# Adding up a body's weighed rows on TensorE, one body later

## The reference

```
comp  = h[src] + rel_emb[rel_id]              # one row of 128 per edge, 474 kinds of relation
score = sum(comp * h[dst], axis=-1)
ex    = exp(score - segment_max(score, dst)[dst])
norm  = ex / segment_sum(ex, dst)[dst]
neigh = segment_sum(comp * norm[:, None], dst)
x     = x + tanh(neigh @ neigh_w)
```

## Time and profile before

| | us |
|---|---|
| median of 3 runs | 10201.28 (10199.97 to 10209.77) |
| the profiled execution | 10194.69 |
| its span, first to last instruction | 10192.9 |
| the last layer's loop, 116 bodies | 8763 to 10131 |

### The profile page before, as it was taken

The page is one execution under the profiler, slowest core; times in us unless marked ns, Lnnn a source line. Parts: engine busy times, 40 slices in busy tenths (PEclk is TensorE's granted clock), DMA queues, the critical chain, the costliest instruction groups (busy, mean ns, idle before and its releaser), DMA issues. The chain is left out here.

```text
span 10192.9 us, 223970 instructions
## 1 busy us (share of the span) xinstructions
PE 6724.1 (66%) x64938; PEld 5458.5 (54%) x64939; DVE 7705.4 (76%) x22255; ACT 5834.0 (57%) x12496; POOL 6563.4 (64%) x5757
## 2 busy tenths in 40 slices
PE   3893986366665666656666478778878876466665
PEld 2882985254554554545555355555555533466664
DVE  9779776477776777767777699989989931677776
ACT  4224226366665666646666389979979920355543
POOL 0777750277776777767777568768858811666665
PEclk8555556578877788877888799999999988777777
DMA  0110115432222322223222212112112264222222
GB/s 23 55 45 15 60 41 197 145 52 53 53 53 44 52 53 53 52 45 52 53 53 53 49 47 59 52 47 59 52 46 59 59 209 162 47 46 46 46 46 44
DMA packets 422026, 630.49 MB, mean 62 GB/s; under 512 B 275527, under 2 KB 332321, under 8 KB 398217
## 3 DMA queue, kind: packets, MB, share of 16 engines
q0 software_dynamic: 192432, 385.10, 18.1%
q1 hardware_dynamic: 162096, 158.87, 5.0%
q10 hardware_dynamic: 67401, 85.32, 2.4%
HBM read 527.43 MB, written 103.02 MB: 62 GB/s over the span
## 5 line engine op out<-in xcount | busy, mean ns | idle before, releaser
L895 POOL DMA_INDIRECT l_land<-table,l_words x3744 | 3598.5, 961 | 1343.2 <-issue 1167.9
L1700 POOL DMA_INDIRECT ell<-gat_stage_pay,gat_stage_at x816 | 1697.1, 2080 | 248.7 <-issue 248.7
L1379 PE MATMUL left_product_ps<-k_w,messageT 128*128 128x128 f32 x5616 | 1035.2, 341 | 529.3 <-ACT messageT L1414 529.3
L1379 PEld LDWEIGHTS left_product_ps<-k_w,messageT 128*128 128x128 f32 x5616 | 872.8, 237 | 734.3 <-ACT messageT L1414 734.3
L2250 PE MATMUL rel_ps<-relation_parts,hot 128*128 128x128 bf16 x11328 | 823.6, 247 | 419.5 <-DVE hot L2349 419.5
L1797 ACT COPY gat_probT<-gat_ps 128x512 f32<-128x512 f32 (+1 forms) x2100 | 1015.3, 551 | 74.8 <-PE gat_ps L1740 66.0
L1373 PE MATMUL left_turned_ps<-ident,message 128*128 128x128 f32 x2808 | 559.1, 334 | 751.5 <-DVE message L1505 751.2
L2250 PEld LDWEIGHTS rel_ps<-relation_parts,hot 128*128 128x128 bf16 x11328 | 803.2, 114 | 441.1 <-DVE hot L2349 441.1
L244 POOL DMA_INDIRECT ell<-pay,position x816 | 841.9, 1032 | 290.4 <-issue 281.2
L1430 ACT ACTIVATE weighed<-kept,l_prob 128x128 f32 x2784 | 888.9, 391 | 59.1 <-ACT l_prob L961 58.9
L1373 PEld LDWEIGHTS left_turned_ps<-ident,message 128*128 128x128 f32 x2808 | 385.8, 173 | 853.9 <-DVE message L1505 850.7
(11 more groups left out here) (332 smaller groups left out, 15746.0 us busy)
## 6 DMA issues: line engine op xcount, KB each, us to landing
gcn_edges<-counts SPq DMA_DIRECT2D x50, 1600.0 KB, 8.1
l_land<-table,l_words POOLq DMA_INDIRECT x3744
rows<-low_dram SPq DMA_DIRECT2D x34, 1536.0 KB
counts<-pair_turned_sb ACTq DMA_DIRECT2D x12, 3200.0 KB, 9.4
logs<-pair_logs ACTq DMA_DIRECT2D x12, 3200.0 KB, 18.2
ell<-pay,position POOLq DMA_INDIRECT x816
ell<-gat_stage_pay,gat_stage_at POOLq DMA_INDIRECT x816
l_words<-ell SPq DMA_DIRECT2D x476, 8.0 KB
```

The source lines that it names most:

```text
L895: pool.indirect_dma_start(self.land[:, p, s, :], None, table[:, :], bass.IndirectOffsetOnAxis(ap=self.words[:, p, s, 0:1], axis=0)).then_i ...
L1379: mm = pe.matmul(right_ps[:, k * H + j, :], messageT[:, k, j, :], k_w[:, :], start=True, stop=True)
L1700: pool.indirect_dma_start(c.ells[1][:, :], bass.IndirectOffsetOnAxis(ap=stage_at[n % 2][:, t:t + 1], axis=0), stage_pay[n % 2][:, t, :], N ...
```

## The change

`Softmax.add` is no longer called in this layer. PE adds the 8 slots of `weighed` in PSUM (`add_up`: 8 float32 matmuls of the identity with `weighed[:, s, :]` into `l3_sum_ps`). It does so for body i-1 in its loop's turn i, behind `widen_kinds(i + 3)` and ahead of `relations(i + 2, ...)`; turn 0 is written out before the loop, and the sum of the last body comes behind it. DVE folds the sum of body n-1 in during body n, behind the 8 score products and ahead of the maximum (`fold`, `Softmax.add_sum`): copy the maximum, sum up `prob`, one operation `denom * keep + part`, and, after a wait for `sum_ready`, one operation `total * keep + weighed_sum`. The end of a block (`finish_block`) and the clearing of the sums are moved to the first body of the next block, behind that fold, under `If`s. A semaphore `score_free` keeps the score products of body n behind the exponentials of n-1; `sum_used` keeps `add_up` behind the fold of the sum before.

```diff
+    def add_sum(self, v, total, weighed_sum, sum_ready, n, sum_used):
+
+        V = self.nc.vector
+        v.wait_ge(self.prob_ready, n)
+        V.tensor_copy(self.top_now[:, :], self.top_new[:, :])
+        V.tensor_reduce(self.part[:, :], self.prob[:, :, :].rearrange("p s h -> p h s"), AX.X, ALU.add)
+        v.drain()
+        V.scalar_tensor_tensor(out=self.denom[:, :], in0=self.denom[:, :], scalar=self.keep[:, 0:1], in1=self.part[:, :],
+                               op0=ALU.mult, op1=ALU.add)
+        v.wait_ge(sum_ready, n)
+        V.scalar_tensor_tensor(out=total[:, :], in0=total[:, :], scalar=self.keep[:, 0:1], in1=weighed_sum[:, :],
+                               op0=ALU.mult, op1=ALU.add).then_inc(sum_used, 1)
...
+                def add_up(n):
+
+                    pe.wait_ge(sum_used, n + 1)
+                    for k in range(HALVES):
+                        pe.wait_ge(weighed_ready[k], n + 1)
+                    for s in range(S):
+                        mm = pe.matmul(sum_ps[:, :], c.ident[:, :], weighed[:, s, :], start=(s == 0), stop=(s == S - 1))
+                    mm.then_inc(sum_ready, 1)
...
-                with pe.Fori(0, all_bodies) as i:
+                widen_kinds(3)
+                for k in range(HALVES):
+                    relations(2, k)
+                with pe.Fori(1, all_bodies) as i:
                     widen_kinds(i + 3)
+                    add_up(i + (-1))
                     for k in range(HALVES):
                         relations(i + 2, k)
+                add_up(all_bodies + (-1))
...
                         kinds(n + 3)
                         soft.mark(c.iota_row)
+                        v.drain()
+                        v.wait_ge(soft.score_free, n + 1)
                         for s in range(S):
                             V.tensor_tensor_reduce(product[:, s, :], comp[:, s, :], h_now[:, :], op0=ALU.mult, op1=ALU.add,
                                                    scale=1.0, scalar=0.0, accum_out=soft.score[:, s, :])
+                        with v.If(n > 0):
+                            fold(n)
+                        with v.If(i < 1):
+                            with v.If(b > 0):
+                                finish_block((b + (-1)).with_bounds(min_val=0, max_val=NB - 1))
+                            soft.clear()
+                            V.memset(total[:, :], 0.0)
                         v.drain()
                         soft.scores(v)
                         for k in range(HALVES):
                             compose(n + 1, k)
                             hots(n + 2, k)
-                        for k in range(HALVES):
-                            v.wait_ge(weighed_ready[k], n + 1)
-                        soft.add(v, weighed, total, part, D)
-                        v.drain()
...
+                fold(all_bodies)
+                finish_block(NB - 1)
```

More of the change, by code:

```diff
@@ L927, in __init__ @@
         self.prob_ready = top.sem(f"{name}_prob_ready")
+        self.score_free = top.sem(f"{name}_score_free")
     def begin(self, degree):
@@ L2199, in composed_attention @@
         h_now = sb("h_now", [P, D])
-        total, part = sb("l3_total", [P, D]), sb("l3_sum", [P, D])
+        total = sb("l3_total", [P, D])
         scale, present = sb("l3_scale", [P, 1]), sb("l3_present", [P, NB])
@@ L2208, in composed_attention @@
         line_ready, line_out = sem("line_ready3"), sem("line_out3")
+        sum_ready, sum_used = sem("l3_sum_ready"), sem("l3_sum_used")
         hot_ready, rel_ready = halves("hot_ready3"), halves("rel_ready3")
@@ L2214, in composed_attention @@
             rel_ps = banks.enter_context(nc.psum_tensor("rel3_ps", [P, S, D], F32))
+            sum_ps = banks.enter_context(nc.psum_tensor("l3_sum_ps", [P, D], F32))
             @block.sync
@@ L2276, in _ @@
                 act.sem_inc(line_out, 1)
+                act.sem_inc(soft.score_free, 1)
                 for k in range(HALVES):
@@ L2321, in _ @@
                 stream.open(v)
+                v.sem_inc(sum_used, 1)
                 V.memset(relation[:, PARTS - 1, :], 0.0).then_inc(relation_blank, 1)
@@ L2372, in _, with fold, finish_block @@
                 v.wait_ge(weights_in, 16)
[L2373 to L2377, removed]
-                    v.drain()
[L2379 to L2385, removed]
-                        v.drain()
-                        soft.scores(v)
-                        for k in range(HALVES):
-                            compose(n + 1, k)
-                            hots(n + 2, k)
-                        for k in range(HALVES):
-                            v.wait_ge(weighed_ready[k], n + 1)
-                        soft.add(v, weighed, total, part, D)
-                        v.drain()
+                def fold(n):
+                    soft.add_sum(v, total, sum_ps, sum_ready, n, sum_used)
+                def finish_block(b):
+                    v.drain()
                     V.tensor_scalar(soft.denom[:, :], soft.denom[:, :], 1.0, None, ALU.max)
@@ L2404, in _ @@
                     v.drain()
+                with v.Fori(0, NB) as b:
+                    many, _, first = stream.block(v, b)
+                    V.tensor_copy(soft.left[:, :], c.degs[1][:, bass.ds(b, 1)])
+                    V.tensor_copy(h_now[:, :], h[:, bass.ds(b, 1), :].rearrange("p a d -> p (a d)"))
+                    v.drain()
+                    with v.Fori(0, many) as i:
+                        n = v.snap(first + i)
+                        kinds(n + 3)
+                        soft.mark(c.iota_row)
+                        v.drain()
+                        v.wait_ge(soft.score_free, n + 1)
+                        for s in range(S):
+                            V.tensor_tensor_reduce(product[:, s, :], comp[:, s, :], h_now[:, :], op0=ALU.mult, op1=ALU.add,
+                                                   scale=1.0, scalar=0.0, accum_out=soft.score[:, s, :])
+                        with v.If(n > 0):
[5 more added lines that the diff above has]
+                            V.memset(total[:, :], 0.0)
+                        v.drain()
+                        soft.scores(v)
+                        for k in range(HALVES):
+                            compose(n + 1, k)
+                            hots(n + 2, k)
+                fold(all_bodies)
+                finish_block(NB - 1)
         project(nc, top, z, c, "neigh_p", 1, D, weights_in, 16,
```

## The result

| | before | after |
|---|---|---|
| median, us | 10200.62 (10190.6 to 10209.77, 4 runs) | 10345.71 (10339.84 to 10348.5, 4 runs) |
| span of the profiled execution | 10192.9 | 10346.7 |
| ratio to before | | 1.0142, 95% interval 1.0128 to 1.0157 |

What follows compares the result with a forecast made beforehand. DVE set the pace before at 11.78 us a body; after, a closed serial loop: 11.48 + 0.36 = 11.84 at full clock, + 1.44 for the low clock = 13.28, +174 us over 116 bodies, 10375 us, range 10310 to 10460.

Steps and rivals of the forecast that it cites:

- the clock was to stay near 0.8: Sign in the profile after: PE's clock in the last layer's loop stays near 0.8, from 0.79 before.
- The closed loop: Last layer's loop: everything from tiles over PE's additions and DVE's fold back to tiles is serial, 11.48 us at full clock.
- First operation of the scores to PE: From DVE's first scores operation to PE's first of the 96 matmuls: 3.00 us, same code after the change.
- The 96 and `line_ps`: PE's 96 relation matmuls and the `line_ps` behind them, at full clock: 5.37 and 0.45 us.
- `total` to the scores: DVE's operation on `total` to the first of the scores: 0.45 us, bounds 0.3 and 0.9.
- Block end: `finish_block` comes into the loop at 24 block ends: 1.73 us more each, 0.36 us a body.
- The additions to DVE: Start of PE's `add_up` to DVE's operation on `total`: 1.54 + 0.67 = 2.21 us.
- The clock: The 96 start at the low clock behind PE's hole, no shorter than before; loss stays 1.44 us a body.
- Rival A: DVE stays the bound and PE's additions hide: -172 us, 10030 us; chance 0.03.
- B: PE's clock stays at 2.4 GHz since its busy share rises: +7 us, 10208 us; chance 0.06.
- C: `line_ps` and `add_up` pay for the low clock too, or it falls twice: +0.65 us a body, 10450; chance 0.20.
- D: A float32 product against the identity takes one record: 0.9 us less, 10271 us; chance 0.06.

Runs made afterwards that it cites:

- e1: Changed kernel with PE adding up body i between the two halves of its 96 matmuls in the same turn; ratio 0.9984 to the kernel before.
- e2: Changed kernel with PE's additions ahead of `line_ps`, not behind it; ratio 1.0060 to the kernel before, 12.27 us a body.
- e8: The changed kernel unedited, on another chip where PE's instructions came with holes; ratio 1.0490 to the kernel before there, 20.90 us a body.
- e4: Changed kernel with only 2 of the 8 slots added up on PE; ratio 1.0050 to the kernel before, 12.09 us a body.
- e3: Changed kernel with 32 unread bf16 matmuls behind the additions, in PE's hole; ratio 1.0026 to the kernel before, 11.97 us a body.
- e5: Changed kernel, additions between the halves of the 96, ACT's exponentials and weighing ahead of its `line_ps` move; slow-fed chip; ratio 1.0123, again 1.0114.
- e6: Kernel before, with ACT's exponentials and weighing ahead of its move of `line_ps`; slow-fed chip; ratio 0.9929, again 0.9929.
- e7: Changed kernel with DVE reducing the weighed rows in the moved fold and no additions on PE; slow-fed chip; ratio 0.9955, again 0.9961.

## Why the prediction was right

The direction, the mechanism and the range held; the period was 13.28 in the prediction and is 12.95. Of the signs that were to show it, one failed: the clock was to stay near 0.8 and was 0.88. By its steps:

- **The closed loop** (tiles, 96, `line_ps`, additions, fold, scores, `compose`, tiles) is there in every body; e1 and e2 changed only its order and moved the time, e8 only its speed. At full clock a turn is 5.81 (9411.14 to 9416.95) + 2.05 (to 9419.00) + 0.44 + 2.98 us (9408.16 to 9411.14) = 11.28, by the rows above; the sum was 11.48.
- **First operation of the scores to PE**: 2.98 us, predicted 3.00. **The 96 and `line_ps`** at full clock: 5.81, predicted 5.37 + 0.45. **`total` to the scores**: 0.44, predicted 0.45; the operation that reads PSUM takes 347 ns and costs nothing unforeseen. **Block end**: 2.09 - 0.44 = 1.65, predicted 1.73.
- **The additions to DVE** is the one mis-sized term: 2.05 us (9416.95 to 9419.00), predicted 2.21. The 16 records take 2.00 us, where scaling the projection's row gave 1.38 + 0.67 = 2.05. DVE starts 0.05 us behind the end of the last record (9416.95 + 2.00, 9419.00), and behind the projection it was 0.16 (10142.42 + 1.38, 10143.96). That is the other 0.11; why the step is shorter here is open.
- **The clock**: 799.4 us over 116 bodies are 6.89 us, 1.36 over 5.53; predicted 1.44. The size was right, the reason only in part. Not every run of 96 behind a wait starts at the low clock, as the prediction had it: 28 of 116 took 5.53 us from the first on (22 of 116 before). I had argued that a hole no shorter leaves the loss as it was, and e4 has the same hole with 0.47 us more. That the loss came out near 1.44 all the same was in part luck.

```profile
L2266 PE MATMUL rel_ps<-relation_parts,hot 128*128 128x128 bf16 x11136 | 799.4, 245 | 442.1 <-DVE hot L2382 442.1
...
L2276 PE MATMUL l_sum_ps<-weighed,ident 128*128 128x128 f32 x1856 | 232.4, 278 | 0.0
```

The differences, 0.20 in the terms at full clock, 0.02 for the block ends and 0.08 for the clock, make 0.30 of the 0.33 us a body that the forecast was high, 38 us in 115 bodies. Against it stand 8 us behind the last body, which I had not counted.

- **Rival A** (DVE stays the bound) is ruled out by its wait of 535 us. **B** (the clock holds) too: 0.88 in the loop, and the 96 at 6.89 us. But e3 shows how much B is worth: with the hole half filled the loop is 1 us shorter. My argument for "no shorter hole, same clock" was wrong on the clock's mean: it rose from 0.79 to 0.88. **C** (`line_ps` and the additions pay for the low clock too) is ruled out: the additions cost 232.4 us over 116 bodies, 2.00 us each, which is what the row at full clock has. **D** is ruled out by 1856 records.

What stays open: why PE was fed so slowly on the one chip, and whether e5's order, on a chip that feeds PE without holes, brings the 10.3 to 10.9 us a body that I expect of it. The best that was shown is ACT's reordering in the kernel before, 0.7% faster, twice, on the slow-fed chip only; e1 is 0.16% faster than before on the other one.

## What to carry to other kernels

Before work is handed to an engine that waits, see at which place of its queue it waits, and who waits behind the handed work: idle time ahead of a burst doesn't help work that comes behind the burst. If the result goes back to the engine that feeds the burst, add up the whole circle, not each engine's load; two engines that wait for each other once in every turn are that circle in the profile. And in such a circle the clock of TensorE is paid in full, so that e3's useless matmuls were worth 1.2% of the kernel.

## What the runs showed of the hardware

- Taking work from PE raised the price of what was left, and adding work lowered it. With 12 of 16 addition records gone, the 96 relation matmuls went from 6.89 to 7.36 us a body and the loop's clock from 0.88 to 0.80; with 32 matmuls added they went to 5.89 and 0.96.
- On one of the chips PE's instructions came in ones to fours every 0.7 or 1.4 us in parts of a burst, at 13.5 us for 96 matmuls in place of 6.7, and the kernel before took 13039 us in place of 10200 (12948 on the second visit; none of its 28 runs there was under 12915). The mean durations of DVE's and ACT's main operations in the loop were the same to a nanosecond. A comparison across chips would have been worth nothing; the ratio to the same kernel on the same chip held for e6 to 0.0000 and for e5 and e7 to 0.001 between two visits.
- VectorE's fused operation on `total` (two tensors of 128 float32 columns and a factor for each partition) took 347 ns with one tensor in PSUM, and 345 in e7 with both in SBUF. So it is not PSUM that makes it dearer than the plain sum of two such tensors, 0.29 us:

```profile
L974 DVE SCALAR_TENSOR_TENSOR l_total<-l_total,l_keep,l_sum_ps x116: 346/347/350, 8790.2 to 10281.9; 128x128 f32<-128x128 f32 x116
```

```profile
L974 DVE SCALAR_TENSOR_TENSOR l_total<-l_total,l_keep,l_sum x116: 338/345/349, 11166.1 to 12896.7; 128x128 f32<-128x128 f32 x116
```
